# Graph transformer layer: the edge one-hot made by VectorE from target numbers in SBUF instead of by TensorE transposes and ScalarE copies

## What is computed

```python
h = (x @ W).reshape(n, H, F)
e = leaky_relu(a_src[src] + a_dst[dst], 0.2)
ex = exp(e - m[dst])
denom = segment_sum(ex, dst)
msg = h[src] * (ex / (denom[dst] + 1e-16))[..., None]
out = segment_sum(msg, dst).reshape(n, H * F) + bias
```

## Time and profile before

| what | us |
|---|---|
| time, median of 3 | 3565.35 |
| span of the profiled execution | 4403.2 |
| edge stage in it, first to last weigh | 211 to 3100 |
| VectorE busy in the whole span | 2365.2 (54%) |
| GpSimd busy | 2160.0 (49%) |
| TensorE busy | 3041.5 (69%) |
| ScalarE busy | 1275.7 (29%) |

### The profile page before, as it was taken

One profiled execution on the slowest core, in us unless ns is written; L12 is line 12 of the kernel. 1 busy time (PEld: TensorE's weight loads), 2 busy tenths in 40 slices (PEclk: granted clock), 3 DMA queues, 4 the chain that ended last, 5 costly groups with the idle time before them and its releaser, 6 DMA issues. The chain is left out here.

```text
span 4403.2 us, 70224 instructions
## 1 busy us (share of the span) xinstructions
PE 3041.5 (69%) x17326; PEld 2470.3 (56%) x17327; DVE 2365.2 (54%) x6486; ACT 1275.7 (29%) x4257; POOL 2160.0 (49%) x2117
## 2 busy tenths in 40 slices
PE   6566666666676776666666777676323349999998
PEld 5444545545555554455555555555323349999997
DVE  7544444444444444545555555555788865555554
ACT  6422222222222222222222222222455523333332
POOL 3255555555555555444444544444066644444444
PEclk9778777878888887878888888888555559999999
DMA  7544444444444444444444444444455724444443
GB/s 262 173 117 117 111 115 112 119 108 111 109 119 111 115 114 117 121 126 121 128 126 122 133 126 125 126 120 111 127 169 186 238 96 71 72 70 72 70 71 55
DMA packets 384652, 529.69 MB, mean 120 GB/s; under 512 B 64276, under 2 KB 323559, under 8 KB 384218
## 3 DMA queue, kind: packets, MB, share of 16 engines
q0 software_dynamic: 114496, 265.49, 25.5%
q1 hardware_dynamic: 185112, 183.84, 14.8%
q10 hardware_dynamic: 84770, 77.19, 5.5%
HBM read 394.80 MB, written 132.72 MB: 120 GB/s over the span
## 5 line engine op out<-in xcount | busy, mean ns | idle before, releaser
L1133 POOL DMA_INDIRECT rows<-node_rows,index x1552 | 1480.9, 954 | 1392.6 <-SPq L1102 930.3
L1411 PE MATMUL ps_sum<-msg,hot 128*128 128x260 f32 x3904 | 1220.7, 465 | 40.0 <-issue 27.9
L1411 PEld LDWEIGHTS ps_sum<-msg,hot 128*128 128x128 f32 x3904 | 853.5, 230 | 198.4 <-issue 45.3
L1391 PE MATMUL ps_hot<-ident_h,hotT 128*128 128x128 bf16 x1952 | 223.5, 247 | 729.7 <-ACT hot L1293 338.6
L1391 PEld LDWEIGHTS ps_hot<-ident_h,hotT 128*128 128x128 bf16 x1952 | 154.3, 110 | 832.8 <-issue 549.4
L1213 DVE TENSOR_TENSOR msg<-rows,ps_w 128x1024 f32<-128x1024 f32 x488 | 596.1, 1222 | 45.1 <-ACT ps_w L1305 29.1
L2140 POOL DMA_INDIRECT out_dram<-big x204 | 352.7, 1729 | 438.3 <-DVE big L2232 390.9
L1195 DVE TENSOR_REDUCE e<-ps_tgt 128x32 f32<-128x96 f32 x488 | 123.3, 253 | 801.2 <-remote 728.2
L1293 ACT ACTIVATE hot<-ps_hot 128x512 f32<-128x512 bf16 x488 | 290.2, 595 | 736.3 <-remote 589.0
L2166 PEld LDWEIGHTS x_ps_hT<-x_rowsT,x_w_now 128*128 128x128 f32 x3264 | 398.0, 192 | 11.5 <-DVE x_w_now L2210 1.1
L2166 PE MATMUL x_ps_hT<-x_rowsT,x_w_now 128*128 128x128 f32 x3264 | 399.1, 276 | 0.7 <-DVE x_w_now L2210 0.7
(11 more groups left out here) (289 smaller groups left out, 4194.9 us busy)
## 6 DMA issues: line engine op xcount, KB each, us to landing
targets<-dst_row SPq DMA_DIRECT2D x391, 128.0 KB
big<-expert_in SPq DMA_DIRECT2D x204, 130.0 KB
rows<-node_rows,index POOLq DMA_INDIRECT x1564
node_rows<-big SPq DMA_DIRECT2D x14, 924.0 KB
turned<-rT SPq DMA_DIRECT2D x14, 896.0 KB, 4.6
area<-turned ACTq DMA_DIRECT2D x98, 128.0 KB
queries<-area ACTq DMA_DIRECT2D x98, 128.0 KB
area<-queries ACTq DMA_DIRECT2D x98, 128.0 KB
```

Of the source, the lines that this page charges most:

```text
L1133: g.indirect_dma_start(rows[:, j, k, :], None, s.node_rows, bass.IndirectOffsetOnAxis(ap=index[:, b, j * G + k:j * G + k + 1], axis=0)).th ...
L1391: mm = pe.transpose(ps_hot[:, k * P:(k + 1) * P], hotT[:, j % 2, k * P:(k + 1) * P], ident_h[:, :])
L1411: mm = pe.matmul(ps_sum[:, j % 2, 0:SUM], hot[:, j % MSGS, k * P:(k + 1) * P], msg[:, j % MSGS, k, :], start=(k == 0), stop=(k == G - 1))
```

## The change

`turn_hot` on TensorE and `copy_hot` on ScalarE are taken out, with the PSUM tensor `ps_hot`. A new input, `dst_cols`, has the target numbers laid out so that edge p of every group of 128 is on partition p. It is copied in DRAM in `project` like the other lists, and SyncE loads all of it into SBUF (`dst_all`, 128 x 1584 int16) ahead of the first `targets`. A new VectorE step, `hot_rows`, at lag 1, makes `hot` directly. For group g and column m it tests whether `dst_all` minus the first node number of the window on this partition's scale (`node_id`) equals `lane_gap`, which is m minus the partition. `target_scores` now waits for `hotT` itself, which `turn_hot` did before. The wait for the sum of the pair four back moves from ScalarE to VectorE.

```diff
 def project(...):
+                g.dma_start(s.dst_cols[:, :], dst_cols[:, :]).then_inc(edges_copied, 16)
...
-                g.wait_ge(edges_copied, 32)
+                g.wait_ge(edges_copied, 48)
...
 def attend_edges(...):
+        dst_all = sb("dst_all", [P, COLS], I16)
+        lane_gap = sb("lane_gap", [P, P])
...
                 fetch_index(1)
+                sp.dma_start(dst_all[:, :], s.dst_cols.rearrange("(p c) o -> p (c o)", p=P)).then_inc(cols_in, 16)
                 for q in range(RING):
                     fetch_targets(q)
...
-                v.tensor_copy(ident_h[:, :], s.ident[:, :]).then_inc(table_ready, 1)
+                v.tensor_scalar(lane_gap[:, :], s.row_iota[:, :], s.part_id[:, 0:1], None, ALU.subtract).then_inc(gap_set, 1)
...
+                def hot_rows(n, j):
+                    column = v.snap(columns[j % 2], min_val=0, max_val=(SUPERS - 1) * G)
...
+                    from_item(v, sum_psum, n, MSGS, n - (MSGS - 1))
+                    v.scalar_tensor_tensor(hot[:, j % MSGS, :].rearrange("p (g n) -> p g n", g=G),
+                                           dst_all[:, bass.ds(column, G)].unsqueeze(2).to_broadcast([P, G, P]), plan.node_id[:, n:n + 1],
+                                           lane_gap[:, :].unsqueeze(1).to_broadcast([P, G, P]), ALU.subtract, ALU.is_equal).then_inc(hot_ready, 1)
...
-                in_pairs([own_row, one_hot, fold, add_sum, score, leaky, weigh, look_up], [0, 1, 2, 6, 2, 2, 3, 0],
+                in_pairs([own_row, one_hot, fold, add_sum, hot_rows, score, leaky, weigh, look_up], [0, 1, 2, 6, 1, 2, 2, 3, 0],
...
-                def copy_hot(n, j):
-                    act.wait_ge(turned, n + 1)
-                    from_item(act, sum_psum, n, MSGS, n - (MSGS - 1))
-                    act.activation(hot[:, j % MSGS, :], ps_hot[:, 0:SPAN], ACT.Copy).then_inc(hot_ready, 1)
...
-                in_pairs([bound, copy_hot, weights], [1, 0, 1],
+                in_pairs([bound, weights], [1, 1],
...
-                def turn_hot(n, j):
-                    pe.wait_ge(hotT_ready, n + 1)
-                    from_item(pe, hot_ready, n, 1, n)
-                    for k in range(G):
-                        mm = pe.transpose(ps_hot[:, k * P:(k + 1) * P], hotT[:, j % 2, k * P:(k + 1) * P], ident_h[:, :])
-                    mm.then_inc(turned, 1)
...
+                    pe.wait_ge(hotT_ready, n + 1)
                     from_item(pe, tgt_folded, n, 1, n)
...
-                in_pairs([turn_hot, target_scores, sum_pair], [0, 0, 3],
+                in_pairs([target_scores, sum_pair], [0, 3],
```

More of the change, by code:

```diff
@@ L101, in allocate @@
     s.dst_placed = nc.dram_tensor("dst_placed", [P * COLS, 1], I16).ap()
+    s.dst_cols = nc.dram_tensor("dst_cols", [P * COLS, 1], I16).ap()
+    s.cols_placed = nc.dram_tensor("cols_placed", [P * COLS, 1], I16).ap()
     s.mixed = nc.dram_tensor("mixed", [NP, D], F32).ap()
@@ L189, in in_turn, with project @@
                 step(n - lag[k])
-def project(nc, s, x, src_table, dst_row, dst, W, att_src, att_dst, gat_bias, w_norm1, w_qkv):
+def project(nc, s, x, src_table, dst_row, dst_cols, dst, W, att_src, att_dst, gat_bias, w_norm1, w_qkv):
     with ExitStack() as ctx:
@@ L703, in place_chunk @@
                         one_hot(c)
-                        from_item(v, scattered[1 - u], c, 1, turn * 32 + 32 * u)
+                        from_item(v, scattered[1 - u], c, 1, turn * 48 + 48 * u)
                         v.tensor_copy(src_now[:, :], every_src[:, bass.ds(c, 1)]).then_inc(placed_parts, 1)
@@ L1016, in attend_edges @@
         hotT_ready = sem("c_hotT_ready")
-        turned = sem("c_turned")
+        cols_in = sem("c_cols_in")
+        gap_set = sem("c_gap_set")
         hot_ready = sem("c_hot_ready")
@@ L1171, in _ @@
                 arrivals = [v.alloc_register(f"arrival{k}") for k in range(2)]
-                unused = v.alloc_register("unused")
+                columns = [v.alloc_register(f"column{k}") for k in range(2)]
                 needed = v.alloc_register("needed")
@@ L1178, in look_up @@
                 def look_up(n, j):
-                    v.load([slots[j % 4], windows[j], arrivals[j % 2], unused],
+                    v.load([slots[j % 4], windows[j], arrivals[j % 2], columns[j % 2]],
                            plan.entry[n // PAIR_RING:n // PAIR_RING + 1, 4 * j:4 * j + 4])
@@ L2252, in program @@
         with stage(nc):
-            project(nc, s, x, src_table, dst_row, dst, W, att_src, att_dst, gat_bias, w_norm1, w_qkv)
+            project(nc, s, x, src_table, dst_row, dst_cols, dst, W, att_src, att_dst, gat_bias, w_norm1, w_qkv)
         with stage(nc), ExitStack() as plan_ctx:
@@ L2305 @@
     inputs["dst_row"] = edges["dst"].astype(_np.int16).reshape(COLS * P, 1)
+    inputs["dst_cols"] = edges["dst"].astype(_np.int16).reshape(COLS, P).T.reshape(COLS * P, 1)
     inputs["L0_ffn_b1"] = _np.asarray(inputs["L0_ffn_b1"]).reshape(EXPERTS * HC, P).T
```

24 lines of the change are left out of this document (14 added, 10 removed).

## The result

The changed kernel takes 3685.4 us (median of 4 runs, 3680.07 to 3688.84), against 3568.2 us for the kernel before in the same comparison. The ratio is 1.0328, with a 95% interval of 1.0312 to 1.0344. I forecast 3659 us, in a range of 3580 to 3705.

What follows compares the result with a forecast made beforehand. GpSimd's gathers were taken to bound the first phase, a VectorE and TensorE loop the second, by a small margin. Terms 58 + 30 + 5 + 1 = +94 us on 3565 gave 3659 us, range 3580 to 3705.

Steps and rivals of the forecast that it cites:

- the rebuilt sum: Whole kernel before, from undisturbed stretches: start 211, phases 1096 and 886, tail about 45, and 1303 give 3541 us.
- (a): `hot_rows` on VectorE, 488 times: 686 ns each, lengthening a turn by 0.62 us.
- (b): Transposes and copy removed: the chain before `project_out` loses 0.25 us; ScalarE's 595 ns a pair priced at nothing.
- the 290 that I gave as a sign: Sign expected in the profile after: ScalarE busy 290 us less.
- (c): Second phase: 132 turns without `add_xn` grow, +82 us; 98 with it shorten, -24 us; net +58 us.
- (d): First phase: VectorE's time hidden by gathers, but `hot_rows` with two SBUF inputs holds gathers up, +30 us.
- (e): Edge stage: `hot_rows` on VectorE waits for the sum four pairs back; cost 0.
- (f): Tail and head: last 12 pairs at VectorE's pace +5 us, load of `dst_all` +1 us, the rest 0.
- No change: Rival: all of `hot_rows` falls into waits, gathers being the loop in both phases; 3565 ± 10 us, chance 0.08.
- partly covered: Rival: VectorE's timed turns are shorter, or gathers and VectorE settle beside each other; 3580 to 3610 us, chance 0.13.
- faster: Rival: TensorE at a low clock sets the pace, so removed transposes gain; 3541 us, down to 3490, chance 0.09.
- The harsher blocking of every gather: Rival: every `hot_rows` holds a gather for all its 0.69 us; 3851 us, chance 0.08 for all over 3705.

Runs made afterwards that it cites:

- e8: The kernel before with `project_out` placed ahead of `sum_pair` in TensorE's turn: 3466.2 us, ratio 0.9715.
- e1: The kernel before, unchanged, profiled a second time: span 3565.2 us, time 3566.9 us.
- e2: The kernel before with the VectorE instruction added, writing an unread tile, transposes and copies kept, no wait for the sum: 3678.4 us, ratio 1.0323.
- e10: The changed kernel with `lane_gap` in PSUM and `hot_rows` put off into turns with `add_xn` where one or two turns suffice: 3577.8 us, ratio 1.0017.
- e5: The changed kernel with two PSUM banks for `ps_tgt`, which `target_scores` writes and `fold` reads in turn: 3670.7 us, ratio 1.0282.
- e3: The changed kernel with the four transposes put back on TensorE, their result unread: 3679.9 us, ratio 1.0331.
- e4: The changed kernel with `lane_gap` in PSUM, so `hot_rows` has one input there: 3657.7 us, ratio 1.0279.
- e7: The changed kernel with `project_out` placed ahead of `sum_pair` in TensorE's turn: 3568.3 us, ratio 1.0.
- e9: The changed kernel with `project_out` ahead of `sum_pair` and `lane_gap` in PSUM: 3547.7 us, ratio 0.9933.

## Why the prediction was right, and where it was not

**The bound.** The reading of two phases was right. First phase, gathers: forecast 1096 us, found 1085. Second phase, a loop of VectorE and TensorE: forecast 886 us, found 939. The quickest turns of each kind were as read from the earlier trace rows; many are longer, which the rebuilt sum left out. That this sum still came within 0.7% of the median was in part luck: the second phase was 53 us short, the first 11 and the tail 20 us too long. e8 shows that the loop through `project_out` was the bound, and by more than I thought: without it the phase falls to 835 us, so its margin was 104 us and not 48. The disturbed first profile was rightly set aside (e1).

**(a) and (b), the prices.** `hot_rows` takes 748 ns where I worked out 686, and a turn grows by 0.66 us (2.33 to 2.99) where I took 0.62. ScalarE's saved copies were worth nothing, as forecast (e2). ScalarE is busy 185 us less and not the 290 that I gave as a sign: the copies overlapped their neighbours, so their durations don't all count as busy time.

**(c), second phase, +58 forecast, +80 measured.** The 132 turns without `add_xn` pay: 132 x 0.66 = 87 us. e10 shows that the 98 others hide it. The failed step is the one that said the turn with `add_xn` ends 0.25 us earlier since "the chain loses the 0.25 us from the transposes' start to that of `target_scores`", -24 us. It is 0. The chain does not run through the transposes but through VectorE's `fold` and `add_sum`, for which `sum_pair` waits, 0.85 us after `hotT` (e5); the transposes were hidden beside it (e3). Taking them out did not even bring `target_scores` forward: it waits for `fold` and starts 0.76 us after `hotT`, where it started at 0.66 in the earlier trace rows. In the earlier trace rows the sum starts 1.00 us after `hotT`, and I took that for a queue behind TensorE's own work. Without this step and with 0.66 the term would have been +87, against +80 measured. In the traces the turns without `add_xn` grew by some 91 us in all, and the 33 with both `divide` and `add_xn` became 11 us shorter in sum. Why these did, no run shows.

**(d), first phase, +30 forecast, +26 measured.** The mechanism is shown by e4: with one input in PSUM the 26 us are gone. The Trainium skill's rule, page "SBUF — State Buffer", section "SBUF: two separate sides", that VectorE with two SBUF inputs blocks a GpSimd operation that reads SBUF, is borne out in kind. To the letter it would give, as an estimate, 47 us with my duration and 55 with the 748 ns measured. The trace of the changed kernel bears out the smaller price that I took from the earlier trace rows. A gather that starts while `hot_rows` runs is longer by what is left of the instruction, less 0.12 to 0.13 us: the one 0.14 us after its start has 0.61 us of it left and takes 0.47 us more. Those that start within its first 0.07 us are not held. My estimate took any start in 1.25 us as equally likely, which with 748 ns would give 36 us. The 80 that were held in the first phase lost 25.

**(e), the new wait: 0 forecast.** e2, which lacks it, is as long as the changed kernel, so here it is 0. The waits grow to 40 us once `project_out` stands first (e7, e9); what they cost there is not shown.

**(f), tail +5, found +6.**

**The rivals.** No change, partly covered and faster did not come. The premise of partly covered, that VectorE's turns are shorter in the timed execution, is refuted by e1: the quickest are as in the first profile, and the phase is longer than the sum. The faster one's premise, a low clock of TensorE, is refuted by the undisturbed profile: 0.96 and 0.98 granted in the two phases. The harsher blocking of every gather did not come either: 80 of the 863 of the first phase were held.

## What to carry to other kernels

Here work was moved from engines that waited to the one whose turns were part of the bound. It cost its full time in every turn in which that engine didn't wait, and what it took off the others gave nothing. So count the turns by kind and put new work where the engine waits anyway (e10). Before an edit is priced as shortening a chain, list every semaphore that each step of the chain waits for: the step removed may lie beside another wait (e5). Look at the order of steps on the other engine of the loop too: `project_out` ahead of `sum_pair` alone gave 2.85% (e8), more than anything else tried. Where GpSimd issued gathers at its limit, an instruction of VectorE with two inputs in SBUF slowed them though VectorE's own time was hidden, and one input in PSUM took that away (e4).

## What the runs showed of the hardware that I had not expected

A profiled execution can be 838 us longer than a second one of the same kernel (4403.2 and 3565.2 us), with waits of up to 14 us for which I found no work, while VectorE's `weigh` (1222 and 1221 ns), the gathers (954 and 951 ns) and the quickest turns are the same in both. A gather beside `hot_rows` with two SBUF inputs took up to 1490 ns in place of 949; with one of the inputs in PSUM the longest was 1191 ns, as before the change (1199 ns). A scalar_tensor_tensor with a broadcast int16 input took 748 ns for 512 columns, 62 ns more than the line through its two neighbours of 256 and 1792 columns, whose inputs are of other kinds.
